# Small-head attention: row maxima written into the expanded queries and turned with them, instead of carried as rows by transfers

## The reference, cut to what matters

```python
q = _apply_rope(q, cos, sin)
k = _apply_rope(k, cos, sin)
scores = jnp.einsum('bhqd,bhkd->bhqk', q, k) / jnp.sqrt(jnp.asarray(hd, x.dtype))
scores = jnp.where(causal, scores, jnp.asarray(-jnp.inf, x.dtype))
attn = jax.nn.softmax(scores, axis=-1)
y = jnp.einsum('bhqk,bhkd->bhqd', attn, v)
...
ascores = jnp.einsum('bhqd,xhkd->bhqk', q, ak) / jnp.sqrt(jnp.asarray(C, x.dtype))
ascores = gating[0] * jax.nn.softmax(ascores.astype(jnp.float32), axis=-1).astype(q.dtype)
y = y + jnp.einsum('bhqk,xhkd->bhqd', ascores, av)
```

## Time and profile before

| | |
|---|---|
| median of 3 executions | 1799.46 us (1791.56 to 1806.72) |
| profiled execution | 1797.53 us |
| its span, first to last instruction | 1795.8 us |
| mean granted TensorE clock | 0.944 of 2.4 GHz |
| PE busy | 1603.5 us, 89% of the span |
| DVE, ACT, POOL busy | 56%, 50%, 55% |

### The profile page before, as it was taken

One profiled execution on the slowest core, in us unless ns is written; L12 is line 12 of the kernel. 1 busy time (PEld: TensorE's weight loads), 2 busy tenths in 40 slices (PEclk: granted clock), 3 DMA queues, 4 the chain that ended last, 5 costly groups with the idle time before them and its releaser, 6 DMA issues. The chain is left out here.

```text
span 1795.8 us, 26487 instructions
## 1 busy us (share of the span) xinstructions
PE 1603.5 (89%) x8164; PEld 1241.0 (69%) x8164; DVE 1003.5 (56%) x2630; ACT 899.3 (50%) x1876; POOL 984.1 (55%) x1122
## 2 busy tenths in 40 slices
PE   5597999998768998589999999999999999979996
PEld 4486555555547886467878788787878878757884
DVE  5561556551656336655666665665666566666235
ACT  3112466652212231377777776777777677731230
POOL 2252455541212443378787877778787777812533
PEclk9798699987879999899999999999999999989999
DMA  2200000000134943244545353444435344363834
GB/s 85 100 1 3 2 3 2 3 3 1 37 113 176 327 145 117 76 112 103 121 100 123 76 133 94 106 111 108 114 82 139 89 94 95 84 232 123 322 118 141
DMA packets 312096, 180.24 MB, mean 100 GB/s; under 512 B 281895, under 2 KB 283767, under 8 KB 309568
## 3 DMA queue, kind: packets, MB, share of 16 engines
q1 hardware_dynamic: 300160, 152.81, 30.7%
q0 software_dynamic: 11840, 26.25, 4.7%
HBM read 111.08 MB, written 22.54 MB: 74 GB/s over the span
## 5 line engine op out<-in xcount | busy, mean ns | idle before, releaser
L1331 POOL TENSOR_TENSOR st_prob<-st_prob,st_rinv 128x512 f32<-128x512 f32 x256 | 265.9, 1039 | 174.4 <-DVE st_rinv L1399 174.4
L1335 POOL TENSOR_TENSOR st_plane<-st_prob,st_plane 128x512 f16<-128x512 f32 x256 | 307.5, 1211 | 0.6 <-ACT st_plane L1251 0.6
L1251 ACT ACTIVATE st_plane<-st_prob 128x512 f16<-128x512 f32 x256 | 161.0, 629 | 126.7 <-POOL st_prob L1331 126.5
L1267 ACT ACTIVATE st_prob<-st_score,st_nmax 128x512 f32<-128x512 f32 x256 | 175.0, 684 | 59.9 <-DVE st_nmax L1406 57.2
L1406 DVE TENSOR_REDUCE st_nmax<-st_score 128x1 f32<-128x512 f32 x256 | 174.9, 683 | 40.0 <-PE st_score L114 37.1
L2044 DVE CUSTOM_DVE_ANT_0 st1b_dump<-st1b_score,st1b_maskrow 128x128 f32<-128x128 f32 (+3 forms) x256 | 112.6, 486 | 98.6 <-PE st1b_score L1742 71.7
L1246 ACT ACTIVATE st_pthi<-st_plane_t 128x512 fp32r<-128x512 f16 x256 | 159.6, 623 | 4.2 <-DMA st_plane_t<-st_plane 4.0
L1376 DVE CAST st_ptlo<-st_plane_t 128x512 fp32r<-128x512 f16 x256 | 148.2, 579 | 3.1 <-DMA st_plane_t<-st_plane 3.1
L1899 ACT ACTIVATE st1b_slabs<-st1b_across 128x512 f32<-128x512 f32 (+1 forms) x192 | 90.6, 526 | 91.4 <-PE st1b_across L1761 69.0
L1380 DVE TENSOR_TENSOR st_olo<-st_outp,st_ohi 128x512 fp32r<-128x512 f32 x64 | 44.1, 689 | 164.9 <-ACT st_ohi L1255 164.9
L112 PE MATMUL st_outp<-st_pthi,st_vhi 128*128 128x512 f32 x256 | 104.3, 407 | 29.4 <-ACT st_pthi L1246 28.5
(11 more groups left out here) (380 smaller groups left out, 4051.0 us busy)
## 6 DMA issues: line engine op xcount, KB each, us to landing
st_raw<-in_moe_w SPq DMA_DIRECT2D x40, 768.0 KB, 7.5
sorted_outs<-st_ln_xn SPq DMA_DIRECT2D x62, 256.0 KB, 3.8
st_qraw<-in_gqa_q SPq DMA_DIRECT2D x8, 1024.0 KB, 5.3
st_oraw<-in_gqa_o SPq DMA_DIRECT2D x8, 1024.0 KB, 5.3
rows<-st_ln_xn SPq DMA_DIRECT2D x2, 2048.0 KB, 8.9
st_kvraw<-in_gqa_kv SPq DMA_DIRECT2D x8, 512.0 KB, 3.9
st_plane_t<-st_plane SPq DMA_TRANSPOSE x256, 2.7
st1a_raw<-in_w_attn SPq DMA_DIRECT2D x3, 1024.0 KB, 6.7
```

Of the source, the lines that this page charges most:

```text
L1251: act.activation(plane[t][:, 0:T], prob[:, t, :], ACT.Copy).then_inc(upper_ready, 1)
L1267: act.activation(prob[:, t, :], score[t][:, :], ACT.Exp, bias=nmax[:, slot:slot + 1], accum_out=rsum[:, slot:slot + 1]).then_inc(exp_ready, 1)
L1331: pool.tensor_tensor(prob[:, t, :], prob[:, t, :], rinv[:, slot:slot + 1].broadcast_to([P, T]), ALU.mult).then_inc(norm_ready, 1)
L1335: pool.tensor_tensor(plane[t][:, T:2 * T], prob[:, t, :], plane[t][:, 0:T], ALU.subtract).then_inc(lower_ready, 1)
```

## The change: the second turn carries the maxima

The maximum is written by GpSimd straight into the spare slot of `qe` (high and low), the whole of the pair's `qe` is turned a second time with four transposes, and ScalarE copies all of it over the pair's `qt`. The minus sign moves to `kt`: its two rows are -1 instead of 1. `nsp`, `xrow`, the four row transfers of each pair and their semaphores are gone. `qe` has four buffers in place of two, since a buffer must live until its second turn, and GpSimd clears the two columns of the spare slot when it builds `qe` anew. The adapter's products stay where they are. Some small tiles are declared later than before (other addresses), and `headmask` shares the tile `gatemask`.

```diff
-        qe = [s.sb(f"qe{n}", [P, TB, 2, SL, HD0], F32R) for n in range(2)]
+        qe = [s.sb(f"qe{n}", [P, TB, 2, SL, HD0], F32R) for n in range(4)]
...
-                def shift(u, d, ab):
-                    m = u.pair(d, ab)
-                    wait(sp, shift_copied, m + 1)
-                    wait(sp, copied, 2 * m + 2)
-                    for n in range(4):
-                        at = 64 * (n // 2) + XROW + n % 2
-                        sp.dma_start(qt[at:at + 1, u.slot(d, ab), :].bitcast(F32),
-                                     xrow[ab][4 * n:4 * n + 4, :].bitcast(F32)).then_inc(shift_loaded[ab], 16)
...
-                    src = (qe, ke)[which][ab]
-                    wait(pe, built, 6 * m + 3 + 3 * which)
+                    src = ke[ab] if which else qe[u.q_of(d, ab)]
+                    wait(pe, built, 7 * m + 4 + 3 * which)
...
                     wait(pe, split_ready, 2 * m + 2)
                     wait(pe, copied, 2 * m + 6 if u.has(2) else 4 * NU)
-                    pe.transpose(prep[0:16, 0:P], nsp[ab][:, :, :, :].rearrange("p i s t -> p (i s t)").bitcast(F32), ident[:, :]).then_inc(shift_ready, 1)
+                    src = qe[u.q_of(1, ab)]
+                    for t in range(TB):
+                        last = pe.transpose(prep[:, t * P:(t + 1) * P], src[:, t, :, :, :].rearrange("p h s d -> p (h s d)").bitcast(F32), ident[:, :])
+                    last.then_inc(shift_ready, 1)
...
                     if two < 2:
-                        wait(pe, shift_loaded[two], 64 * (u.unit() + 1))
+                        wait(pe, shift_copied, u.pair(0, two) + 1)
...
                     wait(act, shift_ready, m + 1)
-                    wait(act, shift_loaded[ab], 64 * u.unit(1))
-                    act.activation(xrow[ab][:, :], prep[0:16, 0:P], ACT.Copy, scale=-1.0).then_inc(shift_copied, 1)
+                    act.activation(qt[:, u.slot(1, ab), :], prep[:, :], ACT.Copy).then_inc(shift_copied, 1)
...
-                    wait(pool, turned, 2 * m - 3 + which)
+                    if which:
+                        wait(pool, turned, 2 * m - 2)
+                    else:
+                        wait(pool, shift_ready, m - 3)
...
+                    if not which:
+                        pool.memset(dst[:, :, :, 3, 0:2].bitcast(F32), 0.0).then_inc(built, 1)
...
                     wait(pool, maxed, 8 * m + 8)
-                    wait(pool, shift_ready, m - 1)
-                    pool.tensor_copy(nsp[ab][:, :, 0, :], nmx[ab][:, :, :]).then_inc(split_ready, 1)
+                    top, dst = nmx[ab][:, :, :].rearrange("p i t -> p t i"), qe[u.q_of(1, ab)]
+                    pool.tensor_copy(dst[:, :, :, 3, 0], top).then_inc(split_ready, 1)
                     wait(pool, split_ready, 2 * m + 1)
-                    pool.tensor_tensor(nsp[ab][:, :, 1, :], nmx[ab][:, :, :], nsp[ab][:, :, 0, :].bitcast(F32), ALU.subtract).then_inc(split_ready, 1)
+                    pool.tensor_tensor(dst[:, :, :, 3, 1], top, dst[:, :, :, 3, 0].bitcast(F32), ALU.subtract).then_inc(split_ready, 1)
...
-                    pool.memset(a[:, :, :, 3, 0:2].bitcast(F32), 1.0).then_inc(cleared, 1)
+                    pool.memset(a[:, :, :, 3, 0:2].bitcast(F32), -1.0).then_inc(cleared, 1)
```

More of the change, by code:

```diff
@@ L144, in __init__ @@
             rows = [self.xn[:, t, :] for t in range(NT)]
+        self.ve, self.sd = s.sb("ln_ve", [P, NT]), s.sb("ln_sd", [P, NT])
+        self.ra, self.rb, self.rc = s.sb("ln_ra", [P, NT]), s.sb("ln_rb", [P, NT]), s.sb("ln_rc", [P, NT])
         self.rows = rows
@@ L1003, in gqa_stage @@
         ohi, olo = s.sb("ohi", [P, NU, T], F32R), s.sb("olo", [P, NU, T], F32R)
+        nmax, rsum, rinv = s.sb("nmax", [P, 2 * TB]), s.sb("rsum", [P, 2 * TB]), s.sb("rinv", [P, 2 * TB])
+        flat = s.sb("flat", [P, TB])
         qbank, sbank = s.ps("qbank", [P, T]), s.ps("sbank", [P, T])
@@ L1610, in heads_block @@
     SL = 4
-    XROW = 3 * HD0
     WIDE = [T - kn * P for kn in range(TB)]
@@ L1637, in heads_block @@
         dump = [s.sb(f"dump{n}", [P, T]) for n in range(2)]
-        pairmask, headmask, gating = s.sb("pairmask", [P, 2 * AK]), s.sb("headmask", [GH * AK, P]), s.sb("gating", [P, 1])
+        gatemask = s.sb("gatemask", [GH * AK, P])
+        nmx = [s.sb(f"nmx{n}", [P, 2, TB]) for n in range(2)]
+        rinv = s.sb("rinv", [P, TB * HU])
+        amax, asum, ainv = (s.sb(n, [P, NAG]) for n in ("amax", "asum", "ainv"))
+        pairmask, gating = s.sb("pairmask", [P, 2 * AK]), s.sb("gating", [P, 1])
         score = [s.ps(f"score{n}", [P, 512]) for n in range(2)]
@@ L1645, in heads_block @@
         shift_ready, shift_copied = s.sem("shift_ready"), s.sem("shift_copied")
-        shift_loaded = [s.sem(f"shift_loaded{n}") for n in range(2)]
         across_ready, exp_ready, kept, pv_done = s.sem("across_ready"), s.sem("exp_ready"), s.sem("kept"), s.sem("pv_done")
@@ L1655, in heads_block @@
         NCONST = 4
-        NCLEAR = 8
+        NCLEAR = 10
         ake = slabs[0:2 * AK, 0:NG0 * GH * SL * HD0].rearrange("p (n s d) -> p n s d", s=SL, d=HD0)
@@ L1683, in slot, with q_of @@
                 return (self.n + d) % 4 * 2 + ab
+            def q_of(self, d, ab):
+                return (self.n + d) % 2 * 2 + ab
             def half(self, d=0):
@@ L1701, in _ @@
             def _(sp):
-                for tile, src in ((maskrow[:, T - P:T], "causal"), (pairmask[:, :], "pairmask"), (headmask[:, :], "headmask"), (gating[:, :], "gating")):
+                for tile, src in ((maskrow[:, T - P:T], "causal"), (pairmask[:, :], "pairmask"), (gatemask[:, :], "headmask"), (gating[:, :], "gating")):
                     sp.dma_start(tile, dram[src]).then_inc(c_loaded, 16)
-                def shift(u, d, ab):
-                    m = u.pair(d, ab)
-                    wait(sp, shift_copied, m + 1)
-                    wait(sp, copied, 2 * m + 2)
-                    for n in range(4):
-                        at = 64 * (n // 2) + XROW + n % 2
-                        sp.dma_start(qt[at:at + 1, u.slot(d, ab), :].bitcast(F32),
-                                     xrow[ab][4 * n:4 * n + 4, :].bitcast(F32)).then_inc(shift_loaded[ab], 16)
[L1714 to L1719, removed]
             @block.tensor
@@ L1954, in expand @@
                     src = (q, k)[which][:, bass.ds(n, 1), :, h:h + 2 * HD0].rearrange("p a t (h d) -> p (a t) h d", d=HD0)
-                    dst = (qe, ke)[which][ab]
-                    wait(pool, turned, 2 * m - 3 + which)
+                    dst = ke[ab] if which else qe[u.q_of(d, ab)]
+                    if which:
+                        wait(pool, turned, 2 * m - 2)
+                    else:
+                        wait(pool, shift_ready, m - 3)
                     for slot in ((0, 2), (0, 1))[which]:
                         pool.tensor_copy(dst[:, :, :, slot, :], src).then_inc(built, 1)
-                    wait(pool, built, 6 * m + 3 * which + 1)
+                    wait(pool, built, 7 * m + 4 * which + 1)
                     pool.tensor_tensor(dst[:, :, :, 1 + which, :], src, dst[:, :, :, 0, :].bitcast(F32), ALU.subtract).then_inc(built, 1)
+                    if not which:
+                        pool.memset(dst[:, :, :, 3, 0:2].bitcast(F32), 0.0).then_inc(built, 1)
                 def split(u, ab):
@@ L2097, in _ @@
                 wait(dve, c_loaded, 16 * NCONST)
[L2098 removed]
+                dve.tensor_scalar(gatemask[:, :], gatemask[:, :], gating[0:GH * AK, 0:1], None, ALU.mult).then_inc(gated, 1)
                 wait(dve, ake_step, 2)
```

11 lines of the change are left out of this document (removed).

## The result

| | before | changed |
|---|---|---|
| median | 1797.22 us (5 executions, 1791.12 to 1806.72) | 1784.58 us (5 executions, 1781.04 to 1789.53) |
| ratio, 95% interval | | 0.9931 [0.9909, 0.9953] |
| profiled execution, span | 1797.53, 1795.8 us | 1789.53, 1787.8 us |
| mean granted clock in it | 0.944 | 0.950 |

The changed kernel is faster by 12.6 us or 0.7%. The profiled execution of it is the slowest of its five. The forecast was 1797 in a range from 1785 to 1811. In the experiments' comparisons the kernel before ran 90 times more (mean 1796.8 us, mean clock 0.943) and the changed one 7 times more (median 1785.85).

What follows compares the result with a forecast made beforehand. TensorE's own queue was taken to bound the small-head stage. Removing waits (-14.6 us) and adding second turns (+14.0), nothing elsewhere, gave -0.6 us on 1797.53, called 1797; the 8-in-10 range was 1785 to 1811.

Steps and rivals of the forecast that it cites:

- The sum: Small-head stage: 14.6 us of waits removed, 14.0 us added on TensorE, nothing elsewhere, together -0.6 us; chance 0.5.
- A: Rival: the clock comes back in turns 1 and 14, 10.2 us faster, 1787 us; chance 0.2.
- B: Rival: the clock falls more often in odd turns 3, 5, 7 and 9, 7.4 us slower, 1804 us; chance 0.1.
- the gaps: TensorE's nine waits for row transfers at step 1, eight in even turns and one in turn 1; 14.6 us to be removed.
- Even turns: Even turns of the small-head stage, forecast at about 12.0 us: 11.26 of work plus 0.38 and 0.35 for the second turns.
- The two prices: Cost of second turns in even turns: 0.38 us for transposes at step 5, 0.35 for ScalarE's longer copy from step 2.
- the leftover: Step 1 of even turns: TensorE could wait for VectorE's maximum; taken as nothing, upper end 0.3 us in 8 turns, 2.4 us.
- Odd turns: Odd turns at the full clock, forecast at about 15.4 us: 14.61 plus 0.38 for each of two second turns.
- GpSimd's memsets: A memset of 16 columns per pair, 0.11 us each, taken as nothing; 3.6 us if all were on the path.
- its splits: GpSimd's two splits write eight strided values instead of adjacent ones; nothing on the path, even at 0.3 us.
- C: Rival: TensorE waits for bank `prep` behind ScalarE's longer copies at step 5 and in odd turns, 9.1 us, 1806; chance 0.1.
- D: Rival: at step 1 VectorE's maximum or GpSimd's adapter product replaces the transfer wait; 14.0 us stand alone, 1811; chance 0.1.

Runs made afterwards that it cites:

- e2: The kernel before without the row transfers and the waits for them, so the maximum isn't subtracted: 1782.3 us, ratio 0.9922.
- e1: The changed kernel with four row transfers per pair put back, of constant data into unused rows, and TensorE waiting for them: 1810.8 us, once more 1812.4.
- e7: The kernel before without transfers and waits, three transposes of the identity added behind each transpose of `nsp`, ScalarE's copy kept small: 1786.4 us.
- e6: The changed kernel with ScalarE's two copies of step 2 exchanged, the one to `qt` before the one to `ot`: 1789.1 us.

## Why the prediction was wrong

**The step that failed is the clock.** The sum has no term for it: the prediction said of the falls "So the fall goes rather with the narrow products, and these stay", and left the kernel's clock as it stood. The mean clock went from 0.943 to 0.951, and this is 8.7 of the 11.8 us by the slope of 1.03, and more by a steeper one. The sign that it named for A and B, a clock that differs by more than 0.05 in some turns, came: in the first profile the clock is higher in turns 1, 9, 11, 13 and 14 than in that of the earlier trace rows, and lower in turns 3 and 5.

Rival A was right that the end of the gaps lets the clock recover, and its size (10.2 us, 1787) was near. That it was so near is in part luck. A looked for the recovery in turns 1 and 14, where 5.8 of 10.5 us came in the profiles, the waits that are gone there included. But turn 1 is at 1.00 in two of three profiles of the kernel before, so of the 6 us that A booked there most is scatter, and for turn 14 it took off no idle time, though TensorE is busy for only 11.00 of its 13.21 us; the rest of the gain lies in turn 14, in the odd turns from 7 on, and in even turns that fall before in some executions. And the gaps alone are not enough: e2 has none and keeps 0.945. The gain needs both halves of the change, no gap (e1 has the second turns and 0.943) and the second turns. What it is about them stays open: e7 has their transposes without the long copy, and 0.946. The prediction argued against A that turns 6 and 8 have the gap and stay at 1.00. That was evidence from one profile: the kernel before falls in turns 4 and 6 in its third profile, and e1 in turns 6 and 8 in its first and in 2, 6, 10 and 12 in its second. That the narrow products stay was true, and the falls behind them became fewer all the same. The Trainium skill's rule (TensorE: Matmul & The Clock Gate, "A second HAM failure mode: psum-queue depth-cycling"), which the prediction set beside A, agrees with e1 against the changed kernel, 0.943 to 0.951, where the prediction held the trace to be against it. By itself it doesn't give A's 10.2 us: between the kernel before and e2, where only the gaps go, the clock rose by 0.002.

**The sum on TensorE's queue** (-0.6 us at an equal clock) was about right. The table's rest is -3.1, and with the steeper slope it would be above zero. Its parts, as the turns show them:
- The gaps: 14.6 us forecast, about 12 came back at an equal clock (11.7 in e2). The time of a wait came back less the 0.29 us for which the next one, on VectorE's maximum, holds TensorE.
- Even turns: 12.0 forecast (11.26 + 0.38 + 0.35), 12.28 measured. The two prices held, 0.38 at step 5 and 0.36 at step 3. The missing 0.28 is that wait, the leftover that the prediction took as nothing because VectorE would have gained 0.38 us. It gained 0.25 in turn 8, and e2 waits as long without any gain. The leftover's upper end, 0.3 us a turn, was right.
- Odd turns: 15.37 forecast, 15.07 measured. The second turn before the adapter's products costs 0.10 us instead of 0.38. With 8 such turns this is 2.2 us too much, about what the leftover takes away.
- GpSimd's memsets (0.115 us each), its splits (0.20 and 0.22 us) and the start of the stage showed nothing on the path. The moved addresses were not tested apart.

**B** (more falls) and **C** (the bank as the path at step 5 and in odd turns) didn't come. C's neighbour did, at step 3 of even turns: 0.56 us instead of 0.19, priced as 0.35 more. **D** came only as the 0.3 us of VectorE.

**The range** from 1785 to 1811 ended 0.4 us above the median. It was to reach to A "with 3 us below". That is 1787 less 3, 1784, which would have held the result; 1785 is a slip. Over all 12 executions of the changed kernel the mean is 1784.95 us. So whether the result fell inside 1785 was a matter of chance. That the forecast lay 12 us too high was not: the sum left the clock out.

Two things stay open: what exactly decides over a fall behind the narrow products (pairs of 27.3 and 27.8 us kept the clock in 30 of 36 odd turns, those of 26.8 in 7 of 18, and width helps at most a little), and how much of the gain is the clock's, from 8.7 us upward.

## What to carry to other kernels

When a change closes short waits of TensorE, read the granted clock of several profiles turn by turn, and give the clock a term of its own: here it was worth at least 8.7 of 11.8 us, and the rest was within 3.5 us of nothing. An added matmul costs less than its spacing where weight loads or a wait already fill the time, so price it at each place. Before taking the time of a wait as gained, ask which wait ends next there (here 0.29 us of each went to VectorE's maximum). And when removing a wait makes no gain, as in e6, look at the mean clock before putting the wait back.

## What the runs showed of the hardware that was not expected

Useless work can pay: with 3.5 us of repeated transposes e6 went from 1789.1 to 1786.0 us (means 2.8 apart, standard error 1.0), though the same work in the changed kernel cost its 3.5 us. A row of sixteen 20-column products cut into groups of four costs 13 to 19 us in the whole kernel. Transfers of single rows beside a busy TensorE, 128 of them, cost nothing that shows as long as nobody waits (1786.9 against 1784.6 and 1785.9 us).
